# Transposing the next norm's first 512 tokens in the cross attentions' last batch, and a new order of work in the group attention's last group

## The reference

```python
x = x + L0_attn(layernorm(x))            # 16 heads, causal
x = x + L0_xattn(layernorm(x), ctx)      # 16 heads over 375 context tokens, scores clipped, LayerNorm of the result
x = x + L0_ffn(layernorm(x))             # RMSNorm, 32 query heads on 4 key heads, then a mixture of 32 experts, top 8
x = x + L1_attn(layernorm(x))            # 32 heads, learned bias
x = x + L1_xattn(layernorm(x), ctx)      # RMSNorm, 16 heads over 375 context tokens, a gate
x = x + L1_ffn(layernorm(x))             # silu(x Wg) * (x Wu), times Wd, hidden 2048
```

## Time and profile before

| | us |
|---|---|
| runs before | 2342.6, 2342.82, 2355.39 |
| median of the runs | 2342.82 |
| profiled execution, its own time | 2340.65 |
| span of the profiled execution | 2338.9 |
| TensorE busy | 2148.9 (92%) |
| VectorE / ScalarE / GpSimd busy | 1315.2 / 927.5 / 988.8 |

### The profile page before, as it was taken

The page is one execution under the profiler, slowest core; times in us unless marked ns, Lnnn a source line. Parts: engine busy times, 40 slices in busy tenths (PEclk is TensorE's granted clock), DMA queues, the critical chain, the costliest instruction groups (busy, mean ns, idle before and its releaser), DMA issues. The chain is left out here.

```text
span 2338.9 us, 40615 instructions
## 1 busy us (share of the span) xinstructions
PE 2148.9 (92%) x14955; PEld 1564.0 (67%) x14955; DVE 1315.2 (56%) x2409; ACT 927.5 (40%) x1673; POOL 988.8 (42%) x858
## 2 busy tenths in 40 slices
PE   7989999788999998889999999698989999989998
PEld 7667877577888887533333333276667777769997
DVE  4754677638787877443333333587852666653333
ACT  2432322345455543236666665225542333222221
POOL 2524555446656654216666665365532110012220
PEclk9999999799999999989999999999999999979999
DMA  3011000221121210557666888630021001001110
GB/s 129 34 59 59 28 28 2 77 68 59 55 64 50 68 46 19 190 214 168 144 143 144 223 223 259 199 94 35 2 78 45 28 28 41 1 28 55 54 54 32
DMA packets 56928, 194.41 MB, mean 83 GB/s; under 512 B 8244, under 2 KB 8500, under 8 KB 49844
## 3 DMA queue, kind: packets, MB, share of 16 engines
q1 hardware_dynamic: 36676, 147.45, 18.1%
q0 software_dynamic: 17280, 38.94, 8.6%
q10 hardware_dynamic: 2784, 5.51, 0.7%
HBM read 158.71 MB, written 33.16 MB: 82 GB/s over the span
## 5 line engine op out<-in xcount | busy, mean ns | idle before, releaser
L2383 PE MATMUL bank<-m_ring,m_bT 128*64 x576 | 266.6, 606 | 3.5 <-ACT m_upper L2111 3.4
L2385 PE MATMUL bank<-m_upper,m_bT 128*64 128x512 f32 x576 | 266.7, 606 | 0.0
L2306 DVE SCALAR_TENSOR_TENSOR m_prod<-bank,m_slot_rows,m_silu 64x256 f32<-64x256 f32 x144 | 69.6, 483 | 275.4 <-ACT m_silu L2057 272.8
L2383 PEld LDWEIGHTS bank<-m_ring,m_bT 128*64 128x64 f32 x576 | 73.9, 138 | 142.3 <-issue 142.3
L2029 POOL DMA_INDIRECT m_sum<-m_yb,m_idx x72 | 102.8, 1428 | 138.0 <-DVE m_yb L2317 110.9
L1059 ACT ACTIVATE y_att_p_rows<-bank,y_att_n_top 112x375 f32<-112x375 f32 x128 | 71.6, 572 | 188.5 <-DVE y_att_n_top L1101 188.5
L2111 ACT ACTIVATE m_upper<-m_ring 128x1024 f32 x144 | 143.5, 1046 | 2.9 <-issue 2.8
L2411 PE MATMUL bank<-m_ring,m_aT 128*64 x288 | 135.4, 592 | 0.7 <-DVE m_aT L2323 0.7
L2413 PE MATMUL bank<-m_upper,m_aT 128*64 128x512 f32 x288 | 135.4, 592 | 0.0
L314 PE MATMUL bank<-f_hT_hi,f_w_hi 128*128 128x448 f32 x288 | 110.8, 385 | 16.4 <-POOL f_w_lo L1550 4.8
L1056 ACT ACTIVATE x_att_pT<-x_att_s_clip 125x336 f32<-125x336 f32 x128 | 55.3, 485 | 153.5 <-DVE x_att_s_clip L1095 153.5
(11 more groups left out here) (481 smaller groups left out, 6201.3 us busy)
## 6 DMA issues: line engine op xcount, KB each, us to landing
m_ring<-in_m_w SPq DMA_DIRECT2D x32, 1536.0 KB, 7.9
f_raw<-in_f_wq SPq DMA_DIRECT2D x64, 256.0 KB, 2.6
z_raw<-in_z_w SPq DMA_DIRECT2D x7, 1536.0 KB, 6.5
f_att_wo_raw<-in_f_wo SPq DMA_DIRECT2D x16, 512.0 KB, 4.4
m_sum<-m_slot_rows SPq DMA_DIRECT2D x4, 2048.0 KB, 18.1
x_c_raw<-in_ctxT SPq DMA_DIRECT2D x8, 752.0 KB, 10.5
y_c_raw<-in_ctxT SPq DMA_DIRECT2D x8, 752.0 KB, 9.8
a_raw<-in_a_wqk SPq DMA_DIRECT2D x8, 256.0 KB, 2.6
```

Of the source, the lines that this page charges most:

```text
L2383: pe.matmul(ps_gu[u % 2][0:HP, :], bT[:, n % 2, k, 0:HP], ring[:, bass.ds(slot + at, D)], start=(k == 0), stop=(k == KC - 1))
L2385: o = pe.matmul(ps_gu[u % 2][HP:P, :], bT[:, n % 2, k, HP:P], upper[:, n % 2, at:at + D], start=(k == 0), stop=(k == KC - 1))
```

## The change

First part: `Norm` gets `lead_parts`. With it, the first four tiles (`lead` = 4) are transposed and split in the last batch of the cross attention ahead, into the places where `hT_hi` and `hT_lo` of the next stage will lie. TensorE's `lead(b, t)` transposes into the bank `ps_kv[t % 2]`, ScalarE's `lead_high` and VectorE's `lead_low` follow at places written into the batch. The stage behind skips those tiles. f_norm moreover gets `loads` as z_norm has them: the first two weight pieces of `f_wk` are loaded in x_att, when the last key/value matmul is done.

Second part: in the group attention, from step 27 on, TensorE makes the values ahead of the second half of the output projection and turns step n+1 behind it, and VectorE takes `heads_low` ahead of `add`.

```diff
@@ class Norm
+    def lead_transposes(self, pe, b, bank):
+        pe.wait_ge(self.h_done if self.kind == "ln" else self.y_done, b + 1)
+        for k in range(KC):
+            t = pe.transpose(bank[:, tile(k)], self.y[:, b, tile(k)], self.g.const("ident"))
+        t.then_inc(self.tr_done, 1)
+
+    def lead_high(self, act, b, bank):
+        act.wait_ge(self.tr_done, b + 1)
+        act.activation(self.lead_parts[0][:, :, tile(b)], bank[:, :].rearrange("p (k s) -> p k s", k=KC),
+                       ACT.Copy).then_inc(self.hi_done, 1)
+
+    def lead_low(self, dve, b, bank):
+        dve.wait_ge(self.hi_done, b + 1)
+        dve.tensor_tensor(self.lead_parts[1][:, :, tile(b)], bank[:, :].rearrange("p (k s) -> p k s", k=KC),
+                          self.lead_parts[0][:, :, tile(b)].bitcast(F32), ALU.subtract).then_inc(self.lo_done, 1)
...
             for b in range(tiles_of(0)):
-                self.low(dve, b)
+                if b >= self.lead:
+                    self.low(dve, b)
...
-                transposed_high(b)
+                if b >= self.lead:
+                    transposed_high(b)
...
-        for b in range(at, to):
+        for b in range(max(at, self.lead), to):
@@ cross_attention, SP
+            if clip:
+                sp.wait_ge(kv_mm, UN * B)
             following.load_ahead(sp)
@@ cross_attention, ScalarE, behind exponent(b, h)
+                    if b == B - 1 and clip and h == 3:
+                        following.lead_high(act, 0, ps_kv[0])
+                    if b == B - 1 and h % 4 == 3 and h // 4 + clip < following.lead:
+                        following.lead_high(act, h // 4 + clip, ps_kv[(h // 4 + clip) % 2])
@@ cross_attention, VectorE, clip_batch
                 keys_values(b + 1, 1)
+                lead_low(b, 0)
                 if b >= 2:
                     rows_of(b - 2)
                     add(b - 2)
+                lead_low(b, 1)
                 for j in range(4, 8):
                     clip_scores(b, j)
...
                 keys_values(b + 1, 4)
+                lead_low(b, 2)
                 for j in range(12, 16):
                     clip_scores(b, j)
+                lead_low(b, 3)
                 inverse_sums(b, 0)
@@ cross_attention, VectorE, max_batch: lead_low(b, c) behind turned(b, 4 * c + 3) and keys_values
@@ cross_attention, TensorE
+            def lead(b, t):
+                if b == B - 1:
+                    pe.wait_ge(kv_done, UN * B)
+                    if t >= 2:
+                        pe.wait_ge(following.lo_done, t - 1)
+                    following.lead_transposes(pe, t, ps_kv[t % 2])
+
             def clip_batch(b):
                 scores(b, 0)
                 project_part(b + 1, 0, 8)
+                lead(b, 0)
+                lead(b, 1)
                 if b >= 2:
                     out_rows(b - 2)
                 scores(b, 1)
                 values(b, 0)
                 project_part(b + 1, 8, 15)
+                lead(b, 2)
                 scores(b, 2)
                 values(b, 1)
                 sums(b, 0)
                 project_part(b + 1, 15, 22)
+                lead(b, 3)
                 scores(b, 3)
...
                     turn(b, 4 * c)
                     turn(b, 4 * c + 1)
                     project_part(b + 1, at, at + 2)
+                    lead(b, c)
                     if c == 0 and b:
                         spread(b - 1)
                     turn(b, 4 * c + 2)
@@ group_attention, VectorE
+                if n + 1 >= DEEP:
+                    for u in range(2):
+                        heads_low(n, u)
                 for grp, k, _, to in full_at(n):
                     if to == GQ:
                         add(grp, k)
                 if n % B < 2:
                     output_weights(n // B, n % B)
-                for u in range(2):
-                    heads_low(n, u)
+                if n + 1 < DEEP:
+                    for u in range(2):
+                        heads_low(n, u)
@@ group_attention, TensorE
             for n in range(N):
-                for u in range(2):
-                    turn(n, u)
+                if n < DEEP:
+                    for u in range(2):
+                        turn(n, u)
                 query(unit_a(n))
...
                 for m in softmax_in(n):
                     scores(m)
+                if n + 1 >= DEEP:
+                    values(n)
                 for now in tiles_now:
                     out_rows(*now)
-                values(n)
+                if n + 1 < DEEP:
+                    values(n)
+                elif n + 1 < N:
+                    for u in range(2):
+                        turn(n + 1, u)
                 query(unit_b(n))
@@ program
-            f_norm = Norm(nc, g, "f_norm", x, "ln_rms", eps2=1e-5, w=g.row("ln1_w"), keep=x2, rows=norm_rows, ready=NT - 1)
+            f_raw = nc.alloc_sbuf_tensor_at("f_lead_raw", [P, 2, KC * P], F32, offset=f_raw_at)
+            f_norm = Norm(nc, g, "f_norm", x, "ln_rms", eps2=1e-5, w=g.row("ln1_w"), keep=x2, rows=norm_rows, ready=NT - 1,
+                          arrived=f_raw_in, loads=[(f_raw[:, u, :], a["f_wk"][u]) for u in range(2)],
+                          lead_parts=lead_parts(nc, "f", f_raw_at + 3 * 4 * 2 * KC * P))
...
             z_norm = Norm(nc, g, "z_norm", x, "ln", rows=norm_rows, ready=NT - 1, arrived=z_raw_in,
+                          lead_parts=lead_parts(nc, "z", z_hT_at),
```

More of the change, by code:

```diff
@@ L160, in __init__ @@
     def __init__(self, nc, g, name, src, kind, eps2=0.0, w=None, keep=None, rows=None, ready=0, loads=(),
[L161 removed]
+                 arrived=None, lead_parts=None):
         self.loads, self.arrived = loads, arrived
+        self.lead_parts, self.lead = lead_parts, tiles_of(0) if lead_parts else 0
         self.stack = ExitStack()
@@ L2756, in transposed, with lead_parts @@
 @contextmanager
-def transposed(nc, g, name):
+def transposed(nc, g, name, parts=None):
     with nc.sbuf_tensor(f"{name}_hT_hi", [P, KC, T], F32R) as hi, nc.sbuf_tensor(f"{name}_hT_lo", [P, KC, T], F32R) as lo:
-        g.hT_hi, g.hT_lo = hi, lo
+        g.hT_hi, g.hT_lo = parts or (hi, lo)
         yield
+def lead_parts(nc, name, at):
+    return tuple(nc.alloc_sbuf_tensor_at(f"{name}_lead_{n}", [P, KC, T], F32R, offset=at + 4 * KC * T * i)
+                 for i, n in enumerate(("hi", "lo")))
 @contextmanager
@@ L2924, in program @@
             kT = st.enter_context(nc.sbuf_tensor("f_kT", [P, NG, T], F32))
-            weights = weight_pair(st, "f")
+            assert (nc.sbuf_base + 31) // 32 * 32 == f_raw_at
+            st.enter_context(nc.sbuf_tensor("f_raw_place", [P, 2, KC * P], F32))
+            weights = weight_pair(st, "f", f_raw)
             causal = g.const("causal")[0:S].unsqueeze(1).broadcast_to([S, 4, S])
             rope = (g.const("cos128"), g.const("sin128"), 0)
-            with transposed(nc, g, "f"):
+            with transposed(nc, g, "f", f_norm.lead_parts):
                 with ExitStack() as w:
@@ L2997, in program @@
             acc = st.enter_context(nc.sbuf_tensor("z_acc", [P, KC, T], F32))
-            with transposed(nc, g, "z"), ExitStack() as w:
+            assert (nc.sbuf_base + 31) // 32 * 32 == z_hT_at
+            with transposed(nc, g, "z", z_norm.lead_parts), ExitStack() as w:
                 weights = expert_weights(w, "z", z_raw)
```

11 lines of the change are left out of this document (9 added, 2 removed).

## The result

| | us | runs |
|---|---|---|
| before, median | 2342.78 | 16 |
| after, median | 2327.74 (2316.65 to 2342.04) | 16 |
| ratio of after to before, 95% interval | 0.9934 [0.9917, 0.9950] | |
| profiled execution of after, its own time | 2342.04 | 1 |

The change takes 15.0 us off the median (11.7 to 19.4 by the interval). A second set of four runs of the same kernel, taken later, gave 2327.7 against 2344.57, ratio 0.9917 [0.9893, 0.9941]. One of the 16 runs of before took 6449.13 us; it is left out of the ratio, and the median hardly moves by it.

A forecast was written before the change was run, and what follows sets the result against it. TensorE was taken as the bound, busy 92% of 2338.9 us. Gains of 6.0 + 4.8 + 5.0 + 0.5 less costs of 1.9 + 2.1 gave 12.3, taken as 12: median 2331, range 2323 to 2339.

The forecast's parts named there:

- f_k: start: Boundary into the f_k projection: first matmul starts at 435.3 instead of 440.74, 5.4 us won.
- f_k: clock: First f_k unit: matmuls following the transposes without a gap spend 1.2 us less at half speed, 0.6 us won.
- z: start: Boundary into the last feed-forward: first matmul at 2080.4 instead of 2084.58, 4.1 us won.
- z: clock: First gate/up unit: restarting at 2080.4 can precede the clock's fall; up to 2.2 us more or nothing, 0.7 taken.
- x_att's last batch: Added transposes, copies and lows in x_att's last batch, partly hidden in waits, cost 1.9 us together.
- y_att's last batch: Added transposes and lows in y_att's last batch, transposes priced at 0.75 us each at half clock, cost 2.1 us together.
- out_rows(5), clock: Transposes filling x_att's 2.35 us gap may keep the clock up; 1.5 us at even chance, 0.5 taken over both batches.
- group's tail: Group attention from step 27: the new order cuts TensorE's 7.1 us of waits for oT_lo by 5.0 us.
- rival (3): Slower: a thinner start keeps the clock at half deep into both projections and the gap-free tail; 2346; chance 0.03.
- rival (4): The moved start is taken back at the next fixed point, a weight load or z_acc's clearing; 2342; chance 0.05.
- rival (1): Clock stays at full through one or both last batches; 6 to 8 us more won, 2324; chance 0.13.
- rival (2): Waits only move: group-tail scores wait for turned_low, last batches pay 7 us instead of 4; 2337; chance 0.17.

The follow-up runs named there:

- the half wait: Changed kernel, but ScalarE's high copy of heads 0 to 3 waits from step 27 only for the output product's first half two tiles back; 2328.93 us, ratio 0.9918.

## Why the prediction was right, and where it wasn't

The prediction was 2331, range 2323 to 2339, chance of within 1% 0.95. Measured 2327.74, 3.3 us below the point. The number was right, its terms only in part:

| term | predicted | measured | from |
|---|---|---|---|
| f_k: start | -5.4 | -5.4 | 6.98 to 1.60 |
| f_k: clock | -0.6 | -0.65 | unit 4.04 to 3.39 |
| z: start | -4.1 | -4.1 | 7.54 to 3.48 |
| z: clock | -0.7 | 0 | unit 7.14 to 7.29; means 7.26 without, 7.25 with leads |
| x_att's last batch | +1.9 | 0 | means 37.6 without, 37.5 with leads |
| y_att's last batch | +2.1 | -3.3 | means 44.3 without, 41.0 in the six profiles with the leads in the change's places |
| out_rows(5), clock | -0.5 | in the batch's 0 | 5.2 in 3 of 7, then 3.7 |
| group's tail | -5.0 | -2.7 | 73.66 to 70.92; 70.87 to 68.13 |
| sum | -12.3 | -16.2 | |

The measured sum of 16.2 stands against 15.0 by the medians, well inside the interval. It is a sum over means of profiles; the runs don't prove its terms one by one. It also leaves out the 4.3 us by which the rest of z_exp is longer in both profiles of after than in both of before (last section).

**Right: both boundaries.** The step "tiles 0 to 3 are done before the barrier and the weights lie in SBUF", with the queues of ScalarE and VectorE counted one by one, gave 1.6 and 3.4 us; all profiles of kernels with both leads show 1.59 to 1.60 and 3.48. What the f_k boundary gained in the clock came as the rows said, and so rival (3), a clock that stays at half deep into the projections, didn't come. Nothing was taken back later that the leads account for: of the eight profiles of kernels with leads or idle transposes in y_att, six have a rest of z_exp of 235.3 to 235.4 us, less than before's 236.8, and rival (4) falls here too.

**Wrong: "So 0.2 to 0.3 us of wait stay in the two steps that have a softmax, and none in the last two."** 0.80 stays in four steps. The working counted VectorE's queue and the values, and took ScalarE's copies to start when the values end. They also wait for `y_done`, because oT has two places, and the change moved that very half behind the values. With that wait on the first half only, three waits are 0.17, and the tail is 5.65 us shorter than before's (70.87 to 65.22), somewhat more than the predicted 5.0. The step that failed is the wait: the queue was counted without this semaphore. The term was 2.3 too large.

**Wrong: "Together 2.1 us" for y_att's last batch, and 1.9 for x_att's.** Each instruction was priced at the speed of the profile of before ("0.75 each", at half clock), as if the clock didn't hang on them. It does: the transposes that were to cost 2.1 us keep the turns, scores and output product from half clock for much of the batch, and it gets 3.3 shorter. That is 5.4 us better than forecast, and both batches together with out_rows(5) are 6.8 better. Rival (1) named this mechanism at 0.13 and priced it at 6 to 8 us below the forecast, which is what came, though only in y_att is the clock shown to be the cause. The 17 us less at half clock bring less than their half, since at full clock TensorE soon waits for ScalarE's exponents and VectorE's copies ([0.47 <-ACT y_att_p_rows L1059] above). In x_att the step that failed is the same pricing, by another amount: against the four profiles with the gap open in which out_rows(5) ran at full clock as well (mean 37.16), the six with leads (37.47) pay 0.3 us, not 1.9. The wait for the reciprocals did grow (3.09 us in after, 2.40 before), but the batch stands at half clock for 17 us with the leads in the change's places and for 20 to 24 without. Whether the leads are the cause of that isn't shown. Against rival (1) the prediction held that the clock was down though TensorE was busy for all of 2053 to 2059; but it had fallen before that stretch (0.88 from 2051 to 2052, 0.50 from 2052 on), behind a wait of 0.86 us, and that a busy TensorE doesn't raise it again there says nothing of whether a filled gap would have kept it from falling.

**Wrong by 0.7: the clock at the z boundary.** "Restarting at 2080.4 can come before the fall" didn't happen: the fall lies in the shorter wait, too. The wait that is left (2.42 us) is as long as the one in which the clock fell at f_k (2.47); that row spoke against a gain here, and the prediction didn't use it.

The errors had opposite signs: the tail and the z clock were taken 3.0 too good, the batches with out_rows(5) 6.8 too bad (+3.5 against -3.3). That the point is only 3.3 off is luck: rival (1) came true in substance, and the two misses on the other side hid half of it. Rival (2), batches that pay 7, is off by sign, and in the tail no score waits for VectorE's low piece (922.10 above has no idle time before it).

## What to carry to other kernels

Work that is ready early can pay twice if it goes into a stretch where TensorE is thinly busy: it leaves the next start, and it can hold the clock where it is put, in some places of the stretch more than in others. So price an added instruction in such a stretch by both clock levels, not by the profile's. When an operation moves behind another, list every semaphore that it increments and who waits for it on each engine, buffers with two places above all. And where stages vary from one execution to the next by more than the change is worth, compare stage by stage over several profiles and leave the spans alone.

## What the runs showed of the hardware that I had not expected

Sixteen transposes whose result nobody reads kept TensorE's clock at 1.00 for the first 24 us of a batch, which took 38.94 us; the six profiles without transposes there took 42.4 to 46.1. A wait of 1.07 us on TensorE kept the clock (first matmul 0.47 us), those of 2.42 and 2.47 us at the boundaries lost it, and one of 2.35 us lost it in three profiles of seven.

The rest of z_exp, which the change doesn't touch, takes 235.3, 236.8 or 241.2 us. Two things make the three lengths. The first is the clock near its end: 3.4 us at half clock in the profiles at 236.8 and 241.2, none at 235.3. The second is the pace of the matmuls at a granted clock of 1.00, with the same waits: from one 448-column matmul to the next it is 202.7 to 202.9 ns in ten profiles and 206.6 in the four at 241.2 (after twice, the group's order alone, the f_wk loads alone), over some 1100 matmuls 4.3 us. So a granted clock of 1.00 doesn't mean one speed. The same two paces stand in the program's first stage, where after has 202.6 ns in one profile and 206.6 in the other; there one kernel shows both. In z_exp the three kernels that were profiled twice repeat theirs. Whether the kernel decides it there, so that after pays 4.3 us there, or whether three repeats are chance, stays open. Against the first speaks that the kernel with the half wait, at 235.4, is no faster in the runs than after. The cause of the two paces isn't shown.
